# Queries unnormalised in the scores, with the inverse norm in the exponential of a windowed attention

## The chip, the core and the metric

The kernel runs on one core of one Trainium2 chip. A core has five engines with their own instruction streams: TensorE (PE, matrix products and transposes), VectorE (DVE), ScalarE (ACT, activations by table), GpSimd (POOL) and SyncE (SP, which issues transfers here). They meet through semaphores only. The metric is the device time of one execution in microseconds (us); lower is better.

## The reference

The input is x of 8 batches, 256 tokens and 128 channels. It is normalised over the channels; the result xn goes into two branches, and both are added to x. The first is a causal attention of 16 heads of 64. The second is a stack of six layers on xn:

```
for i in range(6):
    x = attn_layer(shift_tokens(x), Wqkv[i], q_scale[i], k_scale[i], Wo[i]) + x
    x = ffn_layer(shift_tokens(x), ln_g[i], ln_b[i], W1[i], b1[i], W2[i], b2[i]) + x
```

The attention layer of the stack is where the change is. Queries and keys of each head (64 long) are divided by their l2 norm, multiplied by learned scales, and rotated (`q*cos*scale + rotate_half(q)*sin*scale`). A window of 32 queries sees its own 32 keys and the 32 before, with a causal band. The scores are multiplied by 8, go through a softmax over the 64 keys, and weigh the values. The feed-forward layer is a LayerNorm, a product to 2 x 341 columns, a gate by the exact gelu, and a product back to 128.

## The kernel before

There are two stages. The first (to about 335 us) computes the causal branch and is not changed, but for two buffers of x that now lie elsewhere. The second, some 1600 us, is the stack. Its unit is one batch of one layer, 48 in all, and a unit has four groups of four heads: 192 groups. A pipeline written out by hand runs over 192 slots, one group entering per slot. In slot s the engines work on different groups at once: projections of keys, queries and values for group s+4, norms of group s+3 (the rotated queries and keys are moved by SP for group s+2), scores, softmax and weights of group s, weighing of the values and output projection for groups s-1 and s-2. LayerNorm parts come once every four slots and the MLP of two units once every eight: gate products in slots 5, 6 and 7 of a period of eight, the gelus in slot 0, the up products in 1, 2 and 3, the down product in 4. Every engine's `slot` function fixes its order, and waits in it are on semaphores with constant values.

What happens to one group before the change, on which engine:

- TensorE projects keys and queries into PSUM (`keys`, `queries`). ScalarE squares them (`squares`, line 621) and VectorE multiplies them with the rotary tables (`rotate`, lines 1310 and 1311); the queries are rotated after they are squared.
- GpSimd adds the halves of the squares (line 451), adds the rotary products (`rotated`, line 431, into `z_raw`), and multiplies keys and queries with the inverse norms (`normalise`, line 424, into `z_norm`), 512 columns each.
- TensorE sums the squares over the 32 partitions of a head with a block matrix (`norms`, line 958), 512 columns: 256 tokens of queries and 256 of keys. ScalarE takes Ln (line 690) and the exponential of minus one half of it (line 693); VectorE clamps (line 1390).
- SP copies the result in eight transfers into the layout for the scores, `zqk` (line 350).
- TensorE writes mask and scores into `pair_bank`, two banks of PSUM with 4 blocks of 64 keys each for 128 partitions (32 queries of four windows), `windows`, lines 965 and 974. VectorE takes the negative maximum of the eight blocks (line 1289) and adds it (line 1291), ScalarE takes one exponential of 512 columns in place (line 686), VectorE sums (1296), inverts (1298) and weighs (1301). TensorE transposes (line 984), ScalarE copies to `spread` (line 630), and TensorE weighs the values (line 996). ScalarE copies the output to `yt` (`output_out`, line 657), which TensorE projects (line 926).

ScalarE's other work in a slot: the values to SBUF (`values_out`, line 561), gate copies (715), gelus (663, 667) with a table load before (661) and after (681), the LayerNorm's Ln and exponential (636, 639), its squares (650) and gain (644). VectorE's: input split (1315, 1317), residuals (1325, 1345), hidden products (1353), LayerNorm copies (1332, 1337).

## Time and profile before

| | |
|---|---|
| median of 3 runs | 1941.88 us (1940.21 to 1942.47) |
| profiled execution, its own time | 1940.49 us |
| its span | 1938.7 us |
| mean granted TensorE clock | 0.999 of full |
| instructions | 68797 |
| PE busy in the span | 1851.4 us, x27097 |
| DVE, ACT, POOL busy | 1577.9, 1408.8, 1368.8 us |
| stage of the stack, by its scores | 335.8 to 1904.9 us |

Busy time is time in which an engine has at least one instruction under way; instructions on TensorE are pipelined and overlap in the records. "Idle before" is time in which the engine waited, with what ended the wait. A full-precision matmul shows as two records, a transpose as one. An instruction on VectorE or ScalarE can start before the record of the one ahead of it ends.

### The profile page before, as it was taken

The page shows a single profiled execution, that of the slowest core. Times are in us where ns is not written, and L with a number is a line of the kernel's source. Part 1 is how long each engine was busy: PE and PEld are TensorE (multiplying, and loading weights), DVE is VectorE, ACT ScalarE, POOL GpSimd, SP SyncE. Part 2 cuts the span into 40 slices and gives each one's busy share as a digit, 9 for nine tenths or more (in the row PEclk, how much of TensorE's full clock was granted, in tenths as well). Part 3 has the DMA queues.
Part 4 walks back from the last instruction along what each step waited for, and adds up shares of the span by engine and source line. Part 5 has one row for each costly group of instructions (what it writes and reads, how often), then busy time and mean ns, then how long its engine had stood idle before and what let it go on. Part 6 is the DMA issues. An engine that isn't in the chain of part 4 may idle for free.

```text
span 1938.7 us, 68797 instructions
## 1 busy us (share of the span) xinstructions
PE 1851.4 (95%) x27097; PEld 1394.4 (72%) x27097; DVE 1577.9 (81%) x3052; ACT 1408.8 (73%) x2853; POOL 1368.8 (71%) x1455
## 2 busy tenths in 40 slices
PE   6999998999999999999999999999999999999997
PEld 4777765777767777777777677777677776777774
DVE  5776777888888888788888888888888888888875
ACT  5766665677777777877777777778777777777784
POOL 3010025898798787888787987878887879888770
PEclk9999999999999999999999999999999999999999
DMA  4000001444434334334344343443333443433332
GB/s 131 2 1 0 0 0 39 105 105 103 127 85 110 94 101 128 93 93 104 96 104 123 87 107 97 103 126 94 93 103 96 108 120 88 107 96 102 94 98 67
DMA packets 193542, 171.07 MB, mean 88 GB/s; under 512 B 32304, under 2 KB 190168, under 8 KB 193240
## 3 DMA queue, kind: packets, MB, share of 16 engines
q1 hardware_dynamic: 193240, 166.89, 32.9%
q8 instruction: 209, 3.42, 0.8%
q14 instruction: 93, 0.76, 0.1%
HBM read 21.01 MB, written 1.05 MB: 11 GB/s over the span
## 4 chain that ended last, share of the span: by engine, by line
PE 71%; ACT 12%; issue 7%; DVE 4%; POOL 3%; SPq 3%; DMA 0%; ACTq 0%; POOLq 0%; DVEq 0%
PE bank L996 7%; PE bank L958 7%; PE bank L926 6%; PE pair_bank L974 6%; PE bank L1005 5%; PE bank L984 3%; PE bank L1057 3%; PE bank L1006 3%; PE bank L1007 3%; PE bank L1079 3%; ACT sq L621 2%; SPq L350 2%; PE bank L843 2%; PE bank L1071 2%; ACT probs L690 2%
## 5 line engine op out<-in xcount | busy, mean ns | idle before, releaser
L431 POOL TENSOR_TENSOR z_raw<-rot_u,rot_v 128x256 f32<-128x256 f32 x768 | 553.1, 744 | 100.9 <-DVE rot_v L1311 95.6
L424 POOL TENSOR_TENSOR z_norm<-probs_t,z_raw 128x512 f32<-128x512 f32 x376 | 481.8, 1282 | 92.1 <-DVE probs_t L1390 89.1
L1310 DVE TENSOR_TENSOR rot_u<-bank,tabs 128x512 f32<-128x512 f32 x384 | 263.1, 685 | 165.0 <-ACT sq L621 164.6
L451 POOL TENSOR_TENSOR sqs<-sq 128x512 f32<-128x512 f32 x192 | 246.1, 1282 | 90.0 <-issue 89.4
L1005 PE MATMUL bank<-x_high,w_high 128*128 128x256 f32 x768 | 301.2, 392 | 0.2 <-issue 0.2
L686 ACT ACTIVATE pair_bank<-pair_bank 128x512 f32<-128x512 f32 x192 | 111.7, 582 | 220.4 <-DVE pair_bank L1291 220.1
L1311 DVE TENSOR_TENSOR rot_v<-bank,tabs 128x512 f32<-128x512 f32 x384 | 261.4, 681 | 0.0
L621 ACT ACTIVATE sq<-bank 128x512 f32<-128x512 f32 x384 | 225.2, 588 | 49.8 <-PE bank L1007 43.6
L996 PEld LDWEIGHTS bank<-probs_t,v_late 128*64 128x64 f32 x3072 | 155.0, 137 | 144.4 <-issue 144.4
L630 ACT ACTIVATE probs_t<-bank 64x512 f32<-64x512 f32 x384 | 226.7, 590 | 35.7 <-PE bank L984 33.4
L958 PE MATMUL bank<-sqs,consts 128*128 128x512 f32 x384 | 198.8, 599 | 25.0 <-POOL sqs L451 25.0
L1006 PE MATMUL bank<-x_high,w_low 128*128 128x256 f32 x768 | 216.0, 281 | 0.0
L1007 PE MATMUL bank<-x_low,w_high 128*128 128x256 f32 x768 | 216.0, 281 | 0.0
L996 PE MATMUL bank<-probs_t,v_late 128*64 128x64 f32 x3072 | 198.8, 228 | 0.5 <-ACT probs_t L630 0.5
L926 PE MATMUL bank<-yt,wo 128*128 128x256 f32 x768 | 197.6, 380 | 0.0
L996 PE MATMUL bank<-probs_t,v_sb 128*64 128x64 f32 x3072 | 189.5, 222 | 0.0
L1005 PEld LDWEIGHTS bank<-x_high,w_high 128*128 128x128 f32 x768 | 144.6, 188 | 58.4 <-issue 38.9
L690 ACT ACTIVATE probs<-bank,tiny 128x512 f32<-128x512 f32 x188 | 129.2, 687 | 64.7 <-PE bank L958 62.1
L1289 DVE TENSOR_REDUCE nm<-pair_bank 128x8 f32<-128x512 f32 x192 | 132.1, 688 | 49.3 <-PE pair_bank L974 48.1
L1006 PEld LDWEIGHTS bank<-x_high,w_low 128*128 128x128 f32 x768 | 145.2, 189 | 36.9 <-issue 36.9
L974 PE MATMUL pair_bank<-zqk 64*32 64x64 f32 (+1 forms) x12288 | 163.9, 221 | 0.0
L974 PEld LDWEIGHTS pair_bank<-zqk 64*32 64x32 f32 x12288 | 132.7, 105 | 40.6 <-issue 40.4
(183 smaller groups left out, 4543.4 us busy)
## 6 DMA issues: line engine op xcount, KB each, us to landing
zqk<-z_norm SPq DMA_DIRECT2D x1536, 64.0 KB, 2.1
v_late<-v_sb SPq DMA_DIRECT2D x192, 192.0 KB, 2.6
w_qkv<-in_L_ffn_Wqkv SPq DMA_DIRECT2D x18, 512.0 KB, 4.9
v_late<-v_sb SPq DMA_DIRECT2D x192, 32.0 KB, 2.8
wo<-in_L_ffn_Wo SPq DMA_DIRECT2D x24, 128.0 KB, 2.3
w<-in_L_ffn_W SPq DMA_DIRECT2D x12, 170.5 KB, 2.6
z_norm<-in_L_attn_x SPq DMA_DIRECT2D x4, 256.0 KB, 5.5
w_qkv<-in_L_attn_w_kv_up SPq DMA_DIRECT2D x4, 256.0 KB, 5.0
```

The costliest lines, as they stand in the source:

```text
L424: return pool.tensor_tensor(z_norm[:, parity, idx, :, :], rinv(m)[:, idx, :].unsqueeze(1).broadcast_to([P, 2, T]), z_raw[:, parity, idx, : ...
L431: a = pool.tensor_tensor(z_raw[:, parity, idx, half, :], rot_u[:, idx, half, :], rot_v[:, idx, 1 - half, :], ALU.add)
L621: act.activation(sq[:, idx, :, :], src[:, :].rearrange("p (a t) -> p a t", a=2), ACT.Square).then_inc(S[mark], 1)
L926: mm = pe.matmul(B_X[:, 0:T], wo[:, c, :], yt[:, c, :], start=(c == 0), stop=(c == HD // P - 1))
L958: pe.matmul(B_N[:, :], con("blk"), sqs[:, :, :].rearrange("p a t -> p (a t)"), start=True, stop=True).then_inc(S["n_done"], 1)
L974: mm = pe.matmul(bank[a][WIN * tile:WIN * tile + WIN, at + skip:at + KEYS], zqk[rows, g, 0, pair, WIN * j:WIN * j + WIN], zqk[rows, g, 1, ...
L996: mm = pe.matmul(y[:, t, tile % 2, :, :], (v_sb if tile % 2 else v_late)[:, odd, t, f], spread[:, h, tile, :], start=True, stop=True, tile ...
L1005: pe.matmul(dst, w_high[:, j, cols], x_high[:, odd, :], start=True, stop=False)
L1006: pe.matmul(dst, w_low[:, j, cols], x_high[:, odd, :], start=False, stop=False)
L1007: mm = pe.matmul(dst, w_high[:, j, cols], x_low[:, odd, :], start=False, stop=True)
L1310: dve.tensor_tensor(rot_u[:, idx, :, :], src, tabs[:, 2 * idx, :, :], ALU.mult)
L1311: dve.tensor_tensor(rot_v[:, idx, :, :], src, tabs[:, 2 * idx + 1, :, :], ALU.mult).then_inc(S[mark], 1)
```

## The change

- The queries are no longer multiplied with their inverse norm. Rotated queries and keys go into one buffer, `zs`, of four groups; keys are normalised in place; queries go as they are.
- `squares` writes in another order, and GpSimd's sum likewise, so that the queries' sums lie as two blocks of 128 tokens.
- `norms` makes three products: 256 columns for the keys as before, and two in which the queries' squares are the stationary operand (128 x 128) and four columns of the block matrix move. Their result has one column per head and token block, with the queries' tokens along the partitions: 8 columns. Ln, exponential and clamp run on 256 + 8 columns; the clamp of the 8 goes to `q_rinv`, one for each of four groups.
- Since the inverse norm is positive, the softmax's maximum can be taken of the unnormalised scores. VectorE multiplies the 8 negative maxima with the 8 inverse norms (`lift`), in place of adding the maxima to the 512 scores.
- The exponential becomes eight instructions of 64 columns, with `q_rinv` as scale and `lift` as bias.
- ScalarE's order: the output copy goes ahead of the key squares; the gain of every second LayerNorm goes into the slot after the gelus; in the slot of the gelus both gelus go behind the query squares and behind the next group's values copy, which moves there from the next slot's beginning.
- GpSimd has no second `normalise`; SP waits for the rotated queries besides.

```
--- before.py
+++ after.py
@@ -40,6 +40,7 @@
 
 KEYS = 2 * WIN
 TILES = P // WIN
+NORMS = T + 2 * HG
 
 UNITS = DEPTH * NB
 GROUPS = UNITS * G
@@ -143,8 +144,9 @@
         rot_v = sb("rot_v", [P, 2, 2, T])
         sq = sb("sq", [P, 2, 2, T])
         sqs = sb("sqs", [P, 2, T])
-        z_raw = sb("z_raw", [P, 2, 2, 2, T])
-        z_norm = sb("z_norm", [P, 2, 2, 2, T])
+        zs = sb("zs", [P, G, 2, 2, T])
+        q_rinv = sb("q_rinv", [P, G, 2 * HG])
+        lift = sb("lift", [P, 2 * HG])
 
         zqk = sb("zqk", [P, G, 2, 2, T])
         v_sb = sb("v_sb", [P, 2, TT, HD])
@@ -152,14 +154,14 @@
         nm = sb("nm", [P, HG, TT])
 
 
-        x_rows = z_norm.rearrange("p g a b t -> p (g a b t)").rearrange("p (n c) -> p n c", c=P)
-        xn_rows = z_raw.rearrange("p g a b t -> p (g a b t)").rearrange("p (n c) -> p n c", c=P)
+        x_rows = zs[:, 2:4, :, :, :].rearrange("p g a b t -> p (g a b t)").rearrange("p (n c) -> p n c", c=P)
+        xn_rows = zs[:, 0:2, :, :, :].rearrange("p g a b t -> p (g a b t)").rearrange("p (n c) -> p n c", c=P)
         probs = sb("probs", [P, HG, 3 * P])
         probs_t = sb("probs_t", [P, HG, 3 * P])
         scored = probs.rearrange("p h c -> p (h c)")[:, 0:HG * 2 * KEYS].rearrange("p (a k r) -> p a k r", a=2, r=KEYS)
         spread = probs_t.rearrange("p h c -> p (h c)")[:, 0:HG * TILES * KEYS].rearrange("p (h s c) -> p h s c", h=HG, s=TILES)
-        late_ln = probs.rearrange("p h c -> p (h c)")[:, 2 * GW * 2:].rearrange("p (a t) -> p a t", a=2)
-        late_rinv = probs_t.rearrange("p h c -> p (h c)")[:, 2 * GW * 2:].rearrange("p (a t) -> p a t", a=2)
+        late_ln = probs.rearrange("p h c -> p (h c)")[:, 2 * GW * 2:2 * GW * 2 + NORMS]
+        late_rinv = probs_t.rearrange("p h c -> p (h c)")[:, 2 * GW * 2:2 * GW * 2 + NORMS]
         rsum = sb("rsum", [P, HG, TT])
         rrec = sb("rrec", [P, HG, TT])
         yt = sb("yt", [P, HD // P, T])
@@ -173,11 +175,11 @@
 
         def ln_n(m):
 
-            return late_ln if m >= G else gate[:, 0:2, 0:T]
+            return late_ln if m >= G else gate[:, 0, 0:NORMS]
 
         def rinv(m):
 
-            return late_rinv if m >= G else gate[:, 0:2, T:2 * T]
+            return late_rinv if m >= G else gate[:, 1, 0:NORMS]
 
 
         pair_bank = ctx.enter_context(nc.psum_tensor("pair_bank", [P, 2, 512], F32))
@@ -341,13 +343,14 @@
                 if active(s, -2, GROUPS - 2):
 
                     g = (s + 2) % G
+                    sp.wait_ge(S["q_summed"], s + 3)
                     sp.wait_ge(S["zn_ready"], s + 3)
                     if s + 2 < G:
                         sp.wait_ge(S["qk_done"], HG * (STEPS - G + s + 3))
                     for h in range(HG):
                         for half in range(2):
                             to = 64 * (h % 2) + 32 * half
-                            sp.dma_start(zqk[to:to + 32, g, :, h // 2, :], z_norm[32 * h:32 * h + 32, s % 2, :, half, :]).then_inc(S[f"z_in{g}"], 16)
+                            sp.dma_start(zqk[to:to + 32, g, :, h // 2, :], zs[32 * h:32 * h + 32, g, :, half, :]).then_inc(S[f"z_in{g}"], 16)
                 if active(s, -3, GROUPS - 3):
 
                     g, odd = (s + 3) % G, (s + 3) // G % 2
@@ -418,17 +421,17 @@
                 pool.wait_ge(S[high], count)
                 pool.tensor_tensor(w_low[:, :, cols], src[:, :, cols], w_high[:, :, cols].bitcast(F32), ALU.subtract).then_inc(S[done], 1)
 
-            def normalise(m, idx):
-
-                parity = m % 2
-                return pool.tensor_tensor(z_norm[:, parity, idx, :, :], rinv(m)[:, idx, :].unsqueeze(1).broadcast_to([P, 2, T]), z_raw[:, parity, idx, :, :], ALU.mult)
-
-            def rotated(m, parity, idx, prod, mark):
+            def normalise(m):
+
+                z = zs[:, m % G, 1, :, :]
+                return pool.tensor_tensor(z, rinv(m)[:, 0:T].unsqueeze(1).broadcast_to([P, 2, T]), z, ALU.mult)
+
+            def rotated(m, idx, prod, mark):
 
                 pool.wait_ge(S[prod], m + 1)
-                after(pool, "zn_ready", m - 1)
+                after(pool, f"z_in{m % G}", 16 * 2 * HG * (m // G))
                 for half in range(2):
-                    a = pool.tensor_tensor(z_raw[:, parity, idx, half, :], rot_u[:, idx, half, :], rot_v[:, idx, 1 - half, :], ALU.add)
+                    a = pool.tensor_tensor(zs[:, m % G, idx, half, :], rot_u[:, idx, half, :], rot_v[:, idx, 1 - half, :], ALU.add)
                 a.then_inc(S[mark], 1)
 
             def slot(s):
@@ -437,23 +440,21 @@
                     pool.wait_ge(S["pv_done"], STEPS)
                     pool.memset(spread[:, :, :, :], 0.0).then_inc(S["spread_zero"], 1)
                 if one:
-                    rotated(s + 4, s % 2, 1, "k_prod", "k_summed")
+                    rotated(s + 4, 1, "k_prod", "k_summed")
                 if two:
 
                     pool.wait_ge(S["bound_ready"], s + 4)
-                    after(pool, f"z_in{(s + 1) % G}", 16 * 2 * HG * ((s + 1) // G + 1))
                     pool.wait_ge(S["k_summed"], s + 4)
-                    normalise(s + 3, 1)
+                    normalise(s + 3).then_inc(S["zn_ready"], 1)
                 if one:
                     pool.wait_ge(S["k_square"], s + 5)
                     pool.wait_ge(S["q_square"], s + 5)
                     after(pool, "n_done", s + 4)
-                    pool.tensor_tensor(sqs[:, :, :], sq[:, :, 0, :], sq[:, :, 1, :], ALU.add).then_inc(S["sums_ready"], 1)
-                if two:
-                    pool.wait_ge(S["q_summed"], s + 4)
-                    normalise(s + 3, 0).then_inc(S["zn_ready"], 1)
+                    parts = sq.rearrange("p i a t -> p (i a t)").rearrange("p (n a c) -> p n a c", a=2, c=P)
+                    total = sqs.rearrange("p i t -> p (i t)").rearrange("p (n c) -> p n c", c=P)
+                    pool.tensor_tensor(total, parts[:, :, 0, :], parts[:, :, 1, :], ALU.add).then_inc(S["sums_ready"], 1)
                 if one:
-                    rotated(s + 4, s % 2, 0, "q_prod", "q_summed")
+                    rotated(s + 4, 0, "q_prod", "q_summed")
                 for g in range(G):
                     l = layer_begun(s, LAYER - 7 + g)
                     if l:
@@ -618,7 +619,9 @@
             def squares(m, done, src, idx, mark):
                 act.wait_ge(S[done], m + 1)
                 after(act, "sums_ready", m)
-                act.activation(sq[:, idx, :, :], src[:, :].rearrange("p (a t) -> p a t", a=2), ACT.Square).then_inc(S[mark], 1)
+                n = (4, 2)[idx]
+                dst = sq[:, idx, :, :].rearrange("p a t -> p (a t)").rearrange("p (x n c) -> p n x c", x=2, n=n)
+                act.activation(dst, src[:, :].rearrange("p (n x c) -> p n x c", x=2, n=n), ACT.Square).then_inc(S[mark], 1)
 
             def spread_out(n):
 
@@ -671,7 +674,7 @@
                 one, two = active(s, -4, GROUPS - 4), active(s, -3, GROUPS - 3)
                 three, four = active(s, 0, GROUPS), active(s, 1, GROUPS + 1)
                 normed = g == 0 and active(s, 2 * G, 2 * G + GROUPS)
-                if two and s >= 0:
+                if two and s >= 0 and not mlp_slot(s, 17):
                     values_out(s + 3)
                 if s == 1:
                     act.wait_ge(S["spread_zero"], 2)
@@ -683,14 +686,20 @@
                     deviations((s - 8) // G, B_M)
                 if three:
                     act.wait_ge(S["shifted"], s + 1)
-                    act.activation(both, both, ACT.Exp).then_inc(S["raised"], 1)
+                    for a in range(2):
+                        for k in range(4):
+                            at = 4 * a + k
+                            m = act.activation(both[:, a, k, :], both[:, a, k, :], ACT.Exp, bias=lift[:, at:at + 1], scale=q_rinv[:, g, at:at + 1])
+                    m.then_inc(S["raised"], 1)
                 if two:
                     m = s + 3
                     act.wait_ge(S["n_done"], m + 1)
-                    act.activation(ln_n(m), B_N[:, :].rearrange("p (a t) -> p a t", a=2), ACT.Ln, bias=tiny[:, 0:1], scale=LNS).then_inc(S["ln_done"], 1)
+                    act.activation(ln_n(m), B_N[:, 0:NORMS], ACT.Ln, bias=tiny[:, 0:1], scale=LNS).then_inc(S["ln_done"], 1)
                     act.wait_ge(S["ln_done"], m + 1)
                     after(act, "zn_ready", m)
                     act.activation(rinv(m), ln_n(m), ACT.Exp, scale=-0.5).then_inc(S["rinv_ready"], 1)
+                if four:
+                    output_out(s - 1)
                 if one:
                     squares(s + 4, "k_prod", B_K, 1, "k_square")
                 l = layer_begun(s, LAYER - 5)
@@ -703,22 +712,22 @@
                     rotary_tables(l, 0)
                 if g == 3 and active(s, 7, 7 + GROUPS):
                     xc_squares((s - 7) // G)
-                if normed:
+                if normed and s % (2 * G) == G:
                     gained((s - 8) // G)
-                if four:
-                    output_out(s - 1)
+                if s % (2 * G) == 1 and active(s, 9, 9 + GROUPS):
+                    gained((s - 9) // G)
                 for c in range(3):
                     if mlp_slot(s, 13 + c):
                         p = (s - 13 - c) // (2 * G)
                         act.wait_ge(S["gate_done"], 3 * p + c + 1)
                         after(act, "hid_ready", 3 * p + c - 2)
                         act.activation(gate[0:CW[c], c, :], B_M[0:CW[c], :], ACT.Identity, bias=gate_bias[0:CW[c], c:c + 1]).then_inc(S["gate_ready"], 1)
-                session = mlp_slot(s, 16)
-                if session:
-                    gelus((s - 16) // (2 * G))
                 if one:
                     squares(s + 4, "lq_done", B_Q, 0, "q_square")
-                if session:
+                if mlp_slot(s, 16):
+                    if active(s + 1, -3, GROUPS - 3):
+                        values_out(s + 4)
+                    gelus((s - 16) // (2 * G))
                     last_gelus((s - 16) // (2 * G))
                 l = layer_begun(s, LAYER + 6)
                 if l:
@@ -955,7 +964,12 @@
                 if m == 0:
                     pe.wait_ge(S["res_done"], NB - 1)
                 pe.wait_ge(S["sums_ready"], m + 1)
-                pe.matmul(B_N[:, :], con("blk"), sqs[:, :, :].rearrange("p a t -> p (a t)"), start=True, stop=True).then_inc(S["n_done"], 1)
+                pe.matmul(B_N[:, 0:T], con("blk"), sqs[:, 1, :], start=True, stop=True)
+                heads = con("blk").rearrange("p (b a c) -> p a b c", b=2, a=2)[:, :, :, 0]
+                for x in range(2):
+                    dst = B_N[:, T:NORMS].rearrange("p (a b x) -> p x a b", a=2, b=2)[:, x, :, :]
+                    mm = pe.matmul(dst, sqs[:, 0, P * x:P * x + P], heads, start=True, stop=True)
+                mm.then_inc(S["n_done"], 1)
 
             def windows(n, unit, g):
 
@@ -1283,12 +1297,13 @@
             def by_block(a):
                 return a[:, :, :].rearrange("p (a b) x -> p a (b x)", a=2)
 
-            def shift_windows(n):
+            def lift_windows(n):
 
                 dve.wait_ge(S["scores_done"], n + 1)
                 dve.tensor_reduce(by_block(nm), both, AX_X, ALU.max, negate=True).then_inc(S["top_ready"], 1)
                 dve.wait_ge(S["top_ready"], n + 1)
-                dve.tensor_tensor(both, both, by_block(nm).unsqueeze(3).broadcast_to([P, 2, 4, KEYS]), ALU.add).then_inc(S["shifted"], 1)
+                after(dve, "raised", n)
+                dve.tensor_tensor(lift[:, :], nm.rearrange("p h t -> p (h t)"), q_rinv[:, n % G, :], ALU.mult).then_inc(S["shifted"], 1)
 
             def weigh_down(n):
 
@@ -1378,7 +1393,7 @@
                 if g == 3 and active(s, 7, 7 + GROUPS):
                     centred_out((s - 7) // G)
                 if three:
-                    shift_windows(s)
+                    lift_windows(s)
                 if one:
                     rotate(s + 4, 1, B_K, "lk_done", "k_summed", "k_prod")
                 if g == 0 and active(s, 8, 8 + GROUPS):
@@ -1387,7 +1402,9 @@
                     weigh_down(s)
                 if two:
                     dve.wait_ge(S["rinv_ready"], s + 4)
-                    dve.tensor_scalar(rinv(s + 3), rinv(s + 3), 1e12 / ROOT, None, ALU.min).then_inc(S["bound_ready"], 1)
+                    after(dve, "raised", s)
+                    dve.tensor_scalar(q_rinv[:, (s + 3) % G, :], rinv(s + 3)[:, T:NORMS], 1e12 / ROOT, None, ALU.min)
+                    dve.tensor_scalar(rinv(s + 3)[:, 0:T], rinv(s + 3)[:, 0:T], 1e12 / ROOT, None, ALU.min).then_inc(S["bound_ready"], 1)
                 if s == 0:
                     dve.wait_ge(S["wo_done"], NB + 1)
                     dve.tensor_copy(attn[:, NB - 1, :], B_Y[:, 0:T]).then_inc(S["res_done"], 1)
```

## Rows read from the trace of the kernel before

**Rows 1.** The page, part 1: busy time and share of each engine.

```profile
PE 1851.4 (95%) x27097; PEld 1394.4 (72%) x27097; DVE 1577.9 (81%) x3052; ACT 1408.8 (73%) x2853; POOL 1368.8 (71%) x1455
```

**Rows 2.** Busy time, one period: window, us, PE, PEld, DVE, ACT, POOL, clock, DMA.

```profile
988.02:1053.60 65.58, 64.31 (x1036) 48.86 (x1034) 55.26 (x99) 49.79 (x87) 52.60 (x57) 1.00 0.44 118
```

**Rows 3.** Timeline of PE, end of that period: start us, us, engine, line, operation.

```profile
1053.25 0.60 PE L984 MATMUL bank<-consts,probs 128*128 128x128 f32 x4
1053.68 0.38 PE L965 MATMUL pair_bank<-mask_local_b,ident_b 128*128 128x256 bf16 x2
```

**Rows 4.** Timeline of ACT in a slot with a gate copy: columns as in Rows 3.

```profile
1033.80 0.58 ACT L686 ACTIVATE pair_bank<-pair_bank 128x512 f32<-128x512 f32 x1 [2.44 <-DVE pair_bank L1291]
1034.41 0.69 ACT L690 ACTIVATE probs<-bank,tiny 128x512 f32<-128x512 f32 x1
...
1035.66 0.58 ACT L621 ACTIVATE sq<-bank 128x512 f32<-128x512 f32 x1
1036.14 0.59 ACT L657 ACTIVATE yt<-bank 128x512 f32<-128x512 f32 x1
1036.62 0.69 ACT L715 ACTIVATE gate<-bank,gate_bias 128x512 f32<-128x512 f32 x1
1037.19 0.61 ACT L621 ACTIVATE sq<-bank 128x512 f32<-128x512 f32 x1
...
1038.14 1.19 ACT L630 ACTIVATE probs_t<-bank 64x512 f32<-64x512 f32 x2
1040.49 0.58 ACT L686 ACTIVATE pair_bank<-pair_bank 128x512 f32<-128x512 f32 x1 [1.16 <-DVE pair_bank L1291]
```

**Rows 5.** Timeline of DVE in that slot.

```profile
1032.34 0.69 DVE L1289 TENSOR_REDUCE nm<-pair_bank 128x8 f32<-128x512 f32 x1
1033.07 0.70 DVE L1291 TENSOR_TENSOR pair_bank<-pair_bank,nm 128x512 f32<-128x512 f32 x1
...
1034.87 0.68 DVE L1296 TENSOR_REDUCE rsum<-pair_bank 128x8 f32<-128x512 f32 x1
...
1036.02 0.69 DVE L1301 TENSOR_TENSOR probs<-pair_bank,rrec 128x512 f32<-128x512 f32 x1 [0.23 <-DVE rrec L1298]
...
1036.96 0.85 DVE L1345 TENSOR_TENSOR xs<-bank,xs 64x256 f32<-64x256 f32 x2
1037.84 0.69 DVE L1310 TENSOR_TENSOR rot_u<-bank,tabs 128x512 f32<-128x512 f32 x1
...
1039.05 0.68 DVE L1289 TENSOR_REDUCE nm<-pair_bank 128x8 f32<-128x512 f32 x1
```

**Rows 6.** Groups of ACT by form: count, busy us, mean ns, idle before.

```profile
L644 ACT ACTIVATE xh<-xc,gain 128x256 f32<-128x256 f32 x48 | 28.4, 592 | 0.9 <-DVE xc L1337 0.9
...
L650 ACT ACTIVATE xc<-xc 128x256 f32<-128x256 f32 x48 | 19.5, 407 | 0.9 <-DVE xc L1332 0.9
...
L540 ACT ACTIVATE probs<-pair_bank,nm 128x128 f32<-128x128 f32 x64 | 23.5, 367 | 7.9 <-DVE nm L1236 7.9
```

**Rows 7.** Timeline of PE: output projection, then norms.

```profile
1031.81 1.03 PE L926 MATMUL bank<-yt,wo 128*128 128x256 f32 x4
1032.67 1.02 PE L958 MATMUL bank<-sqs,consts 128*128 128x512 f32 x2
```

**Rows 8.** Groups of DVE by form, as Rows 6.

```profile
L1317 DVE TENSOR_TENSOR x_low<-xs,x_high 128x256 fp32r<-128x256 f32 x48 | 61.6, 1284 | 1.7
...
L1325 DVE SCALAR_TENSOR_TENSOR xs<-bank,out_bias,xs 64x512 f32<-64x512 f32 x46 | 34.3, 746 | 4.4 <-PE bank L1175 2.5 <-PE bank L1079 1.6
L1353 DVE SCALAR_TENSOR_TENSOR hid<-bank,out_bias,gate 128x512 f32<-128x512 f32 x44 | 32.9, 747 | 0.7
```

**Rows 9.** Timeline of ACT in the slot of the gelus.

```profile
990.74 0.58 ACT L686 ACTIVATE pair_bank<-pair_bank 128x512 f32<-128x512 f32 x1 [0.37 <-DVE pair_bank L1291]
991.83 0.69 ACT L690 ACTIVATE probs<-bank,tiny 128x512 f32<-128x512 f32 x1 [0.51 <-PE bank L958]
...
1000.89 0.58 ACT L686 ACTIVATE pair_bank<-pair_bank 128x512 f32<-128x512 f32 x1
```

95 lines of the change are left out of this document (56 added, 39 removed).

## The prediction

> **What bounds the kernel now.** I read the page's busy shares first, then one period of the second stage, then the timelines of ScalarE and VectorE in one slot. TensorE is busy for 95% of the span [rows 1]. The second stage is 192 slots in 24 periods of eight (a pair of MLP blocks goes through in eight slots). The period from the mask product at 988.02 to the one at 1053.68 takes 65.66 us [rows 2, 3], and in it TensorE is busy for 64.31 us, VectorE 55.26, ScalarE 49.79 and GpSimd 52.60 [rows 2]. So TensorE sets the pace and the others wait for it in most slots. ScalarE has 16 us per period to spare, 2 us per slot. That is the number to watch, for the change puts seven more instructions per slot on ScalarE.
>
> In a slot without a gelu ScalarE starts the exponential at 1033.80, the Ln at 1034.41, the key squares at 1035.66, and the next exponential at 1040.49, having idled for 1.16 us [rows 4]. VectorE reduces at 1032.34, shifts, sums at 1034.87, weighs at 1036.02, and reduces again at 1039.05: 6.71 us with almost no idle time, 0.88 of them the residual at 1036.96 [rows 5]. These two engines form a ring: exponential, Ln and its exponential, squares of the keys, squares of the queries (ScalarE), rotation of the queries, maximum, shift (VectorE), exponential. Today it has slack against TensorE. The question is its length after the change. I call the time from one slot's first exponential to the next slot's a ring step.
>
> **The exponentials.** One instruction of 512 columns (0.58 us, the next 0.61 after its start) becomes eight of 64, each with a scale and a bias read from SBUF. The trace has no such instruction. The nearest: 128 columns out of PSUM with a bias from SBUF take 367 ns; a 256-column one with both operands takes 592 against 407 with neither, so 93 ns for each operand [rows 6]. 512 columns without either take 0.58 [rows 4], 367 less 93 is 274 for 128, so a column costs 0.80 ns. 64 columns with both: 367 - 51 + 93 = 409 ns. Instructions that follow each other overlap by 0.10 (squares 0.58 long, the next 0.48 later [rows 4]), so they start 0.31 apart, and the eight take 7 x 0.31 + 0.41 = 2.58. Bounds: 0.20 apart, if the operands are read under the instruction before (lower), and 0.41, if nothing overlaps. The upper end is real: the present exponential, the one instruction of ScalarE that writes PSUM, has no overlap with the one behind it (0.61 from start to start [rows 4]). I take 0.31, because 64-column instructions into one bank depend on nothing before them, and every other chained group overlaps.
>
> By the Trainium skill, "ScalarE: Activation LUTs", on what an ACTIVATE costs, an instruction is 186 ns plus 0.833 ns per column plus 93 ns for each pointer operand, and neighbours overlap by 93. An estimate from that is 0.33 apart, 2.75 for the eight; the sum below would be about 2042 by it. The trace agrees on the 93 ns of an operand.
>
> **What is taken off.** Ln and its exponential shrink from 512 to 264 columns, 0.20 each: from Ln to squares 0.84 instead of 1.25 [rows 4]. The shift on VectorE (0.70 from PSUM to PSUM) becomes a product of 8 columns, some 0.20 (at least 0.1, at most the 0.70); the first exponential starts 0.96 after the reduction instead of 1.46 [rows 5]. The clamp becomes two smaller ones, nought net (between -0.2 and +0.1). GpSimd loses the query normalisation, one of its four steps a slot; it has 13 us per period of idle time already [rows 2], and its sums, 1.3 behind the query squares, are wanted only in the next slot. SP keeps its eight transfers per slot, and the added wait on the query sums is met a slot before (they end on GpSimd one slot ahead of the key normalisation that SP waits for anyway), so the transfers start no later.
>
> **TensorE.** The norm product of 512 columns loses its half: four records of 256 columns take 0.86 [rows 7], so 256 columns of full precision are 0.43. In return come two products with 128-column weights and 4 moving columns, two records each: four weight loads. The four transposes of a slot, a load and 128 columns each, take 0.43 from 1053.25 to 1053.68 [rows 3], so a load is at most 0.11. One load lies under the product ahead; 0.33 to 0.36 stays. Net -0.07 per slot (between -0.35 and +0.05). Off TensorE's path this is worth nothing, on it 13 us.
>
> **The ring after the change**, from first exponential to the next, for a bare slot: to the Ln 2.61, Ln and exponential 0.84, output copy 0.48 (now ahead of the squares, on the ring), key squares 0.48, query squares 0.61; that is 5.02. Then rotation 1.21, reduction 0.72, lift 0.24: 7.19. VectorE's own way is 2.62 to the sum (it idles 1.4 behind the key rotation; the exponential used to hide there), then 1.15 to the weighing and 0.75 with the clamp scaled down [rows 5], so at 4.52 it is free, and 2.17 more make 6.69. Extras: gate copy 0.57 [rows 4], residual 0.88 [rows 5], input split 1.7 with its cast, MLP residual 1.53 for two, hidden product 0.66 [rows 8], centred copy 0.35. By slot of the period (0 has the gelus):
>
> - 0: today 10.15, all ScalarE but for a wait of 0.51 [rows 9]; +2.00 for the exponentials, -0.41 Ln, -0.51 wait gone, -0.49 gain [rows 6] moved to slot 1: 10.7
> - 1: 4.52 + 0.88 + 0.66 + 2.17 = 8.2
> - 2: 4.52 + 0.66 + 2.17 + 0.35 = 7.7
> - 3: ScalarE's own load, 2.61 + 0.84, four of 0.48, 0.31 for the centred squares [rows 6], 1.2 for the spread copies [rows 4] and 0.93 for the LayerNorm's Ln and exponential of 256 columns (by the column rate): 7.8
> - 4: 4.52 + 1.7 + 2.17 + 1.53 = 9.9
> - 5, 6: 7.19 + 0.57 = 7.8, and 8.1 with the centred copy
> - 7: the same with a gate copy: 8.4
>
> The sum is 68.6 against 65.66. TensorE's own work is 64.31 [rows 2], so the ring leads and TensorE waits for weights in most slots. 2.9 x 24 = 70 us on the profiled execution's 1940.5 (span 1938.7): 2010, and 1.4 more against the median of 1941.88: **2012**. The first stage doesn't change.
>
> **Sensitivity.** 0.01 us in the spacing is 0.08 in each of the slots, 15 us in all. 0.28 gives 1965, 0.34 gives 2058: the forecast's own range.
>
> **Rivals.**
> 1. *No overlap between exponentials* (0.41 apart, as the present one stands to its successor). Ring +0.8 per slot, +154: about 2165. For it: the 0.61 of rows 4. Against: its successor is another function with a wait of its own.
> 2. *The change is faster.* The operands are fetched under the instruction before, 0.20 apart. Then the ring is 68.6 - 8 x 0.88 = 61.5 per period and TensorE sets it: 64.31 busy [rows 2], less 0.56 for the norms, plus half of the 1.27 that it idles today (the query rotation no longer stands behind the gelus, which is where sums come late): 64.4, -1.3 x 24 = -31: about 1910. It decides below a spacing of 0.26 (2.9 us in eight slots is 0.36 per slot, 0.045 per exponential). For it: VectorE and ScalarE have slack today. Against: the 93 ns of an operand show in the spacing too: behind the gate copy with its bias (0.69 long) the next starts 0.57 later, behind a plain square (0.58) 0.48 later [rows 4].
> 3. *In between*, 0.25 to 0.27: 1940 to 1955, where ring and TensorE tie.
>
> A change that doesn't do what it says (norms not halved in time) is in the TensorE bounds and moves nothing where the ring leads.
>
> **Chances.** Forecast 0.45, rival 1 0.27, rival 2 0.16, rival 3 0.12 (of which 0.05 within 0.2%, 0.01 below). A measurement of this kernel tells 0.2% from no change. Faster 0.17, same 0.05, slower 0.78. The range from 1935 to 2170 leaves out rival 2 and the tail above rival 1.
>
> **What would show it.** In the changed profile: eight exponentials of about 0.41, 0.31 apart; VectorE idle before the sum of the weights (line 1296 now) for some 1.4 us, released by ScalarE, near nil today; TensorE idle before the transposes, released by VectorE's weights; ScalarE over 90% busy; TensorE under 93%. The norm products' step falls from 0.86 to about 0.8. If the exponentials start 0.25 apart or less, or TensorE stays at 95%, the forecast is wrong. If they are 0.40 apart, rival 1 holds. If the period is long with exponentials at 0.31, the ring isn't the cause, and I would look at GpSimd's sums and the values' wait for the Ln.

## The result and the profile after

The changed kernel takes 2051.78 us (median of 4 runs, 2049.37 to 2054.73) against 1941.16 (1940.21 to 1942.47, 4 runs): ratio 1.057, 95% interval 1.0552 to 1.0588. It is slower by 110.6 us; the forecast was 2012, slower by 70. The profiled execution has a span of 2050.4 us at a granted clock of 0.998 of full speed, so the clock plays no part.

The page of the changed kernel, part 1 (busy us, share of the span, instructions; it answers to [rows 1]):

```profile
PE 1864.0 (91%) x27865; PEld 1520.5 (74%) x27865; DVE 1477.5 (72%) x3244; ACT 1668.8 (81%) x4197; POOL 1132.3 (55%) x1263
```

ScalarE gains 260 us of busy time, VectorE loses 100 and GpSimd 236. TensorE is nearly as busy as before in us, but over a longer span: 91% instead of 95%. So it waits more. Part 4 of the same page, the chain that ended last (shares by engine, then by line):

```profile
ACT 38%; PE 30%; DVE 19%; issue 11%; DMA 0%; ACTq 0%; POOL 0%; DVEq 0%; SPq 0%
ACT pair_bank L692 18%; DVE nm L1303 4%; ACT sq L624 3%; PE pair_bank L988 3%; DVE rot_v L1326 2%; DVE rsum L1311 2%; PE bank L1093 2%; PE bank L998 2%; ACT probs L697 2%; ACT probs_t L633 2%; ACT gate L724 2%; DVE hid L1368 2%; PE bank L852 2%; DVE lift L1306 2%; PE bank L1115 2%
```

The eight exponentials (L692) are 18% of that chain, and ScalarE and VectorE together are 57% of it. It is the ring: exponentials, squares, rotation, maximum (L1303), lift (L1306). Part 5 of the page, two of its groups (busy us, mean ns, then idle time before them with what ended it):

```profile
L692 ACT ACTIVATE pair_bank<-pair_bank,lift,q_rinv 128x64 f32<-128x64 f32 x1536 | 469.3, 387 | 143.3 <-DVE lift L1306 143.0
...
L1311 DVE TENSOR_REDUCE rsum<-pair_bank 128x8 f32<-128x512 f32 x192 | 132.7, 691 | 289.9 <-ACT pair_bank L692 289.9
```

An exponential of 64 columns takes 387 ns (409 forecast). VectorE stands idle for 290 us ahead of the sum of the weights, always for the last exponential.

One slot of ScalarE, 1012.52 to 1020.28 (timeline: start us, us, engine, line, operation, count; in brackets the idle time before it and what ended it). It answers to [rows 4]:

```profile
1012.52 2.44 ACT L692 ACTIVATE pair_bank<-pair_bank,lift,q_rinv 128x64 f32<-128x64 f32 x8 [1.91 <-DVE lift L1306]
1015.00 0.48 ACT L697 ACTIVATE probs<-bank,tiny 128x264 f32<-128x264 f32 x1
...
1015.84 0.58 ACT L660 ACTIVATE yt<-bank 128x512 f32<-128x512 f32 x1
...
1016.79 0.69 ACT L724 ACTIVATE gate<-bank,gate_bias 128x512 f32<-128x512 f32 x1
1017.36 0.61 ACT L624 ACTIVATE sq<-bank 128x512 f32<-128x512 f32 x1
...
1020.28 2.45 ACT L692 ACTIVATE pair_bank<-pair_bank,lift,q_rinv 128x64 f32<-128x64 f32 x8 [0.77 <-DVE lift L1306]
```

Eight exponentials take 2.44 us from start to end, so they start (2.44 - 0.39) / 7 = 0.29 apart (0.31 forecast). The next such block starts 7.76 us later, a ring step of slot 5 (7.8 forecast). The other blocks of this period start at 1002.20, 1028.71, 1037.33, 1047.86, 1055.87, 1064.30 and 1072.73. Against the forecast:

| slot | 4 | 5 | 6 | 7 | 0 | 1 | 2 | 3 | sum |
|---|---|---|---|---|---|---|---|---|---|
| forecast | 9.9 | 7.8 | 8.1 | 8.4 | 10.7 | 8.2 | 7.7 | 7.8 | 68.6 |
| measured | 10.32 | 7.76 | 8.43 | 8.62 | 10.53 | 8.01 | 8.43 | 8.43 | 70.53 |

The period was 65.66 [rows 3]. Every fourth period is longer, before and after: a layer begins in it, and it went from 69.3 to 72.76 us (starts of the exponentials in both timelines). Between the first block of exponentials and the one 23 periods later, five of them of the long kind, the kernel grew by 104.3 us (18 times 4.87 and five times 3.4 are 105). With 1.6 ahead of it and 5.7 behind it that is the 111.7 us by which the span grew. The busy times in this period, which answer to [rows 2] (window, us, PE, PEld, DVE, ACT, POOL, clock, DMA share, GB/s):

```profile
1002.20:1072.73 70.53, 64.88 (x1067) 54.03 (x1067) 51.53 (x107) 60.48 (x144) 43.05 (x48) 1.00 0.43 115
```

No engine is full: ScalarE 60.48 of 70.53 (86%; I had said over 90%), TensorE 92%. The time is in their dependence on each other.

The forecast's steps with 2.45 in place of 2.58 for the exponentials would sum to 68.6 - 8 x 0.13 = 67.6. The kernel needs 70.5, so 2.9 us of the period (about 70 us in all) were missing from the forecast. Over the slots as they were forecast, slots 2 and 3 are long by 0.73 and 0.63, slot 4 by 0.42, slot 6 by 0.33 and slot 7 by 0.22. What TensorE waited for tells where (the changed kernel's waits of TensorE; us in total, times, longest):

```profile
PE bank L1031 <- ACT probs L697: 32.6, 29, 2.2
PE bank L1107 <- DVE hid L1368: 29.7, 22, 1.7
PE bank L1010 <- ACT probs_t L633: 21.9, 23, 1.0
PE bank L1107 <- ACT gate L724: 21.2, 23, 1.1
PE bank L1115 <- ACT gate L724: 14.1, 23, 1.9
PE bank L998 <- DVE probs L1316: 13.1, 53, 2.1
```

The largest row is the values' product (L1031). It waits for the Ln in slot 1, behind the gelus of slot 0, and neither of these slots is longer than forecast. I had forecast waits of the transposes (L998) for the weights in most slots; that is the last and smallest row. L1107 and L1115 are the two small LayerNorm products (mean and variance) of slots 2, 3, 6 and 7. They write the PSUM bank that the MLP uses too, so they wait until VectorE has read the hidden product out of it (L1368) or ScalarE the gate (L724). The transposes, the mask and the scores stand behind L1107 in TensorE's order and start only after it. Slot 2, TensorE then VectorE (timelines):

```profile
1061.08 0.67 PE L1107 MATMUL bank<-xs,consts 128*128 128x256 f32 x2 [1.23 <-DVE hid L1368]
1061.59 0.60 PE L998 MATMUL bank<-consts,probs 128*128 128x128 f32 x4
1062.03 0.38 PE L979 MATMUL pair_bank<-mask_local_b,ident_b 128*128 128x256 bf16 x2
1062.34 0.84 PE L988 MATMUL pair_bank<-zqk 64*32 64x32 f32 x64
```

```profile
1058.35 0.69 DVE L1311 TENSOR_REDUCE rsum<-pair_bank 128x8 f32<-128x512 f32 x1 [1.32 <-ACT pair_bank L692]
...
1059.31 0.69 DVE L1316 TENSOR_TENSOR probs<-pair_bank,rrec 128x512 f32<-128x512 f32 x1
...
1060.19 0.75 DVE L1368 SCALAR_TENSOR_TENSOR hid<-bank,out_bias,gate 128x512 f32<-128x512 f32 x1
...
1063.21 0.69 DVE L1303 TENSOR_REDUCE nm<-pair_bank 128x8 f32<-128x512 f32 x1 [0.75 <-PE pair_bank L988]
1063.94 0.32 DVE L1306 TENSOR_TENSOR lift<-nm,q_rinv 128x8 f32<-128x8 f32 x1
```

The late exponentials hold back the sum, the sum the weighing, the weighing the hidden product, and that holds TensorE for 1.23 us. So the scores come late, and VectorE idles another 0.75 for them. That is a second, longer ring through TensorE, which my sum over ScalarE and VectorE didn't have.

The lift has no fixed price either. It is 0.32 here, 0.17 and 0.44 elsewhere; the last section shows what sets it.

### The profile page after: what moved, and what is told of

It is laid out like the page before. It is cut to its first block, busy times and chain, and to the rows that moved or that the text cites. A ratio compares the mean times of both kernels' runs of the same rounds, so it can differ in the third digit from the quotient of the medians.

```text
span 2050.4 us, 72240 instructions
## 1 busy us (share of the span) xinstructions
PE 1864.0 (91%) x27865; PEld 1520.5 (74%) x27865; DVE 1477.5 (72%) x3244; ACT 1668.8 (81%) x4197; POOL 1132.3 (55%) x1263
## 4 chain that ended last, share of the span: by engine, by line
ACT 38%; PE 30%; DVE 19%; issue 11%; DMA 0%; ACTq 0%; POOL 0%; DVEq 0%; SPq 0%
ACT pair_bank L692 18%; DVE nm L1303 4%; ACT sq L624 3%; PE pair_bank L988 3%; DVE rot_v L1326 2%; DVE rsum L1311 2%; PE bank L1093 2%; PE bank L998 2%; ACT probs L697 2%; ACT probs_t L633 2%; ACT gate L724 2%; DVE hid L1368 2%; PE bank L852 2%; DVE lift L1306 2%; PE bank L1115 2%
## 5 line engine op out<-in xcount | busy, mean ns | idle before, releaser
L434 POOL TENSOR_TENSOR zs<-rot_u,rot_v 128x256 f32<-128x256 f32 x768 | 548.7, 736 | 224.8 <-DVE rot_v L1326 221.6
L692 ACT ACTIVATE pair_bank<-pair_bank,lift,q_rinv 128x64 f32<-128x64 f32 x1536 | 469.3, 387 | 143.3 <-DVE lift L1306 143.0
L427 POOL TENSOR_TENSOR zs<-probs_t,zs 128x512 f32<-128x512 f32 x188 | 239.7, 1275 | 373.3 <-DVE probs_t L1407 373.3
L1311 DVE TENSOR_REDUCE rsum<-pair_bank 128x8 f32<-128x512 f32 x192 | 132.7, 691 | 289.9 <-ACT pair_bank L692 289.9
L455 POOL TENSOR_TENSOR sqs<-sq 128x512 f32<-128x512 f32 x192 | 250.4, 1304 | 30.1 <-issue 27.5
L1303 DVE TENSOR_REDUCE nm<-pair_bank 128x8 f32<-128x512 f32 x192 | 131.9, 687 | 56.7 <-PE pair_bank L988 53.3
L1010 PEld LDWEIGHTS bank<-probs_t,v_sb 128*64 128x64 f32 x3072 | 158.7, 138 | 1.0 <-issue 1.0
```

Of the source, the lines that this page charges most:

```text
L427: return pool.tensor_tensor(z, rinv(m)[:, 0:T].unsqueeze(1).broadcast_to([P, 2, T]), z, ALU.mult)
L434: a = pool.tensor_tensor(zs[:, m % G, idx, half, :], rot_u[:, idx, half, :], rot_v[:, idx, 1 - half, :], ALU.add)
L455: pool.tensor_tensor(total, parts[:, :, 0, :], parts[:, :, 1, :], ALU.add).then_inc(S["sums_ready"], 1)
L692: m = act.activation(both[:, a, k, :], both[:, a, k, :], ACT.Exp, bias=lift[:, at:at + 1], scale=q_rinv[:, g, at:at + 1])
L1010: mm = pe.matmul(y[:, t, tile % 2, :, :], (v_sb if tile % 2 else v_late)[:, odd, t, f], spread[:, h, tile, :], start=True, stop=True, tile ...
```

## The experiments

All of them are the changed kernel or the kernel before with one edit. Ratios are against the kernel before on the same chip (1941 to 1942 us).

**1. One exponential.** One instruction of 512 columns again, with a constant scale; the inverse norm and the shift are still computed but not applied.

```diff
-    for a in range(2):
-        for k in range(4):
-            m = act.activation(both[:, a, k, :], ..., ACT.Exp, bias=lift[:, at:at + 1], scale=q_rinv[:, g, at:at + 1])
+    act.activation(both, both, ACT.Exp, scale=1e-30)
```

> The changed kernel with its eight exponentials of 64 columns put back to one of 512, with no bias and no scale from SBUF (a tiny constant scale; the lift and the inverse norm are left out of the softmax). Theory, the exponentials on the ring set the changed kernel's time: without them ScalarE gives back about 1.9 us per slot, the ring falls under TensorE's work, and the time is below before, 1905 to 1930 us. Rival, the slowdown comes from the other parts (SP's added wait, the order of ScalarE, the small products): it stays above 1990 us.

Measured: 1891.75 us (1889.56 to 1894.03), ratio 0.9749 (0.9732 to 0.9765). TensorE is busy for 97% of the span:

```profile
PE 1822.6 (97%) x27865; PEld 1513.3 (80%) x27865; DVE 1470.1 (78%) x3244; ACT 1358.7 (72%) x2853; POOL 1138.9 (60%) x1263
```

It is 13 us below the range that I had given it. The eight exponentials with their operands cost 160.0 us, and all else in the change gives back 49.4. The loss is theirs alone.

This run also shows what a slot costs without the ring. Its slots 3 and 7 take 7.9 and 8.07 us (medians of the periods), and slot 4 takes 10.36, as long as in the change. The same slot 4 in the kernel before, in the changed kernel and in this one (columns as in the window above):

```profile
1023.33:1033.80 10.47, 10.47 (x141) 7.02 (x141) 9.03 (x16) 5.62 (x10) 7.17 (x8) 1.00 0.42 105
```

```profile
1002.20:1012.52 10.32, 10.32 (x144) 8.20 (x143) 8.55 (x17) 6.98 (x18) 5.51 (x6) 1.00 0.38 95
```

```profile
1001.98:1012.36 10.38, 10.38 (x145) 8.25 (x143) 8.44 (x17) 5.32 (x12) 5.49 (x6) 1.00 0.39 101
```

TensorE is busy for all of it in all three. Slot 4 is TensorE's own, whatever the exponentials cost, and the trace before the change showed it: I forecast 9.9 for a slot that took 10.47.

**2. The norm product.** As 1, with the norm product of 512 columns in place of its half and the two small ones (the norms that it gives are then not those wanted).

```diff
-    pe.matmul(B_N[:, 0:T], con("blk"), sqs[:, 1, :], ...)      # and two with 4 moving columns
+    pe.matmul(B_N[:, :], con("blk"), sqs[:, :, :]...)
```

> As one_exp, and with the norm product of TensorE put back to one of 512 columns (the small sums of the queries are then not what they should be). With TensorE as the bound, this measures the norm edit by itself. Theory: the four weight loads of the new products eat what the halved product gives, so the two kernels are within 0.3% (6 us) of each other. Rival, the halving saves its 0.3 us and more per slot: this one is 50 us slower than one_exp.

Measured: 1901.07 us, ratio 0.9796 (0.9779 to 0.9812), so halving is worth 9.3 us where TensorE leads, 0.049 per slot. My theory had allowed 6 and the rival wanted 50: nearer to the theory, but outside of it. TensorE in experiment 1, then in this one (timelines, norm product to the next product):

```profile
1002.51 0.59 PE L963 MATMUL bank<-sqs,consts 128*128 128x256 f32 x2
1002.94 0.50 PE L967 MATMUL bank<-consts,sqs 128*128 128x4 f32 x4
1003.37 0.34 PE L1006 MATMUL bank<-probs_t,v_late 128*64 128x64 f32 x4
```

```profile
1006.25 1.02 PE L963 MATMUL bank<-sqs,consts 128*128 128x512 f32 x2
1007.20 0.34 PE L1001 MATMUL bank<-probs_t,v_late 128*64 128x64 f32 x4
```

0.86 against 0.95 from start to start: the half product takes 0.43 and the small ones, four weight loads for 16 columns, another 0.43.

**3. The order alone.** The kernel before with the change's order of ScalarE (output copy ahead of the key squares, query squares ahead of the gelus, value copy and gain moved).

```diff
+    if four: output_out(s - 1)
     if one: squares(s + 4, "k_prod", B_K, 1, "k_square")
...
-    if session: gelus(...)
     if one: squares(s + 4, "lq_done", B_Q, 0, "q_square")
+    if mlp_slot(s, 16): values_out(s + 4); gelus(...)
```

> The kernel before with ScalarE's new order alone. Theory: the query squares no longer stand behind the long gelu, so the sums come in time and TensorE's wait in the gelu slots shrinks: 1915 to 1935 us, a little faster than before. Rival, the order is a cost of its own (the output copy ahead of the key squares delays the rotation): 1950 us or more.

Measured: 1928.14 us, ratio 0.9935 (0.9918 to 0.9951): 13 us gained. The kernel before and this one, TensorE's wait for GpSimd's sums of squares:

```profile
PE bank L958 <- POOL sqs L451: 25.0, 28, 1.3
```

```profile
PE bank L960 <- POOL sqs L451: 6.4, 6, 1.2
```

The query squares no longer stand behind the gelus, and 18.6 us of this wait go; other waits take back some. This is the gain that rival 2 had named.

**4. Eight exponentials alone.** The kernel before; VectorE's shift goes into the bias, the scale is a tile of ones.

```diff
-    dve.tensor_tensor(both, both, by_block(nm)..., ALU.add).then_inc(S["shifted"], 1)
...
-    act.activation(both, both, ACT.Exp)
+    for a in range(2):
+        for k in range(4):
+            m = act.activation(both[:, a, k, :], ..., ACT.Exp, bias=top[:, at:at + 1], scale=unit[:, at:at + 1])
```

> The kernel before with only its exponential changed: eight of 64 columns, the negative maximum as bias and a column of ones as scale, both from SBUF, and no shift on VectorE. Everything else, norms, normalisation on GpSimd and order, is as before. Theory, the exponentials alone make the slowdown: 2035 to 2090 us (the Ln is longer and the gelu slot is in its old order, so rather above the changed kernel's 2052). Rival, the slowdown needs the other parts: below 1990 us.

Measured: 2071.61 us, ratio 1.0672 (1.0654 to 1.069), 130 us slower, though VectorE is spared 0.70 us per slot. So the exponentials do it without the norms, the order or the rest. They take the same time here (groups of ScalarE: busy us, mean ns):

```profile
L694 ACT ACTIVATE pair_bank<-pair_bank,nm,unit 128x64 f32<-128x64 f32 x1536 | 468.6, 386 | 106.8 <-DVE nm L1299 106.5
```

**5. Eight without operands, and 6. with one.** The changed kernel; the exponentials have a constant scale, with no bias (5) or with the lift as bias (6). The inverse norm isn't applied in either, nor the maximum in 5.

```diff
-    m = act.activation(both[:, a, k, :], ..., ACT.Exp, bias=lift[:, at:at + 1], scale=q_rinv[:, g, at:at + 1])
+    m = act.activation(both[:, a, k, :], ..., ACT.Exp, scale=1e-30)                          # 5
+    m = act.activation(both[:, a, k, :], ..., ACT.Exp, bias=lift[:, at:at + 1], scale=1e-30)  # 6
```

> The changed kernel with its eight exponentials of 64 columns kept, but with a constant scale and no bias, so without operands from SBUF (the lift and the inverse norm are left out of the softmax). By the plain form's own numbers (0.58 us for 512 columns, 0.80 ns a column) one takes 0.22 us and the eight start 0.11 to 0.12 apart, about 1.0 us in all, 1.4 less than with the operands. Theory, the price is the operands' on the ring: 1890 to 1910 us, near one_exp's 1892. Rival, it is the number of instructions: above 1970 us.

> The changed kernel with a constant scale in its eight exponentials, so one operand from SBUF (the bias) instead of two; the inverse norm is left out as scale. The two ends are measured: 2.44 us for eight with both operands (2052 us), and eight without any (1901 us). Theory: each operand adds 0.09 to every start, so these start 0.20 apart, 1.7 us in all, 0.74 less per slot than with both; the ring falls to about TensorE's work: 1910 to 1940 us. Rival, an operand's cost comes once however many there are: 2030 us or more.

Measured: 5 takes 1900.66 us, ratio 0.9788 (0.9772 to 0.9804); 6 takes 1943.15, ratio 1.0004 (0.9994 to 1.0014), 3 us above the range that I had given it. One block of each (timelines of ScalarE), 5 first:

```profile
1016.20 1.02 ACT L692 ACTIVATE pair_bank<-pair_bank 128x64 f32<-128x64 f32 x8 [1.90 <-DVE lift L1306]
```

```profile
1008.31 1.72 ACT L692 ACTIVATE pair_bank<-pair_bank,lift 128x64 f32<-128x64 f32 x8 [1.10 <-DVE lift L1306]
```

1.02, 1.72 and 2.44 us with none, one and two operands: each costs some 0.70 us in eight instructions, 0.09 in one. Being eight costs only 8.9 us of the kernel's time (1891.75 to 1900.66). The first operand costs 42.5 and the second 108.6, though both add about 0.7 x 192 = 135 us to ScalarE: the slack that the ring had against TensorE takes up most of the first and little of the second. The price per instruction is linear, the kernel's time is not.

**7. The MLP's bank freed early.** The changed kernel; the hidden product is read out of its bank ahead of the weighing on VectorE, the gate copy is put ahead of the output copy on ScalarE.

```diff
     dve.reciprocal(...)
+    if mlp_slot(n, 17 + c): hidden_out(p, c, B_M, ...)
     dve.tensor_tensor(scored, ...)
...
+    if mlp_slot(s, 13 + c): act.activation(gate[0:CW[c], c, :], B_M[0:CW[c], :], ...)
     if four: output_out(s - 1)
```

> The changed kernel with bank 3 released earlier: on VectorE the hidden product goes ahead of the weighing, on ScalarE the gate copy goes ahead of the output copy. The LayerNorm's product on TensorE waits for these, and the transposes and scores stand behind it. Theory, in slots 2, 3, 6 and 7 the ring is closed through TensorE by that wait: each gets 0.4 to 0.7 us shorter, 2005 to 2025 us. Rival, only the ring of ScalarE and VectorE counts (as the prediction had it): swapping inside it leaves its length, 2045 us or more.

Measured: 2047.65 us (2041.81 to 2053.84), ratio 1.0548 (1.0518 to 1.0578). A miss: I expected 2005 to 2025, and against the change's 1.057 (1.0552 to 1.0588) the gain isn't clear of the noise. Slots 1 to 3 (ScalarE's timeline; the block after slot 0 starts at 1043.31):

```profile
1051.72 2.45 ACT L692 ACTIVATE pair_bank<-pair_bank,lift,q_rinv 128x64 f32<-128x64 f32 x8 [1.51 <-DVE lift L1306]
1059.44 2.44 ACT L692 ACTIVATE pair_bank<-pair_bank,lift,q_rinv 128x64 f32<-128x64 f32 x8 [0.98 <-DVE lift L1306]
1067.39 2.43 ACT L692 ACTIVATE pair_bank<-pair_bank,lift,q_rinv 128x64 f32<-128x64 f32 x8
```

Slots 2 and 3 fall from 8.43 and 8.43 to 7.72 and 7.95, as the second ring says they should. But slot 1 rises from 8.01 to 8.41. The hidden product starts there at once, and the weights come 0.66 us later for it. What lengthens the slot is the lift: it took 0.19 in the change and takes 0.60 here, up to 1051.68, just behind the end of a GpSimd instruction at 1051.66 (timelines of VectorE and GpSimd; the last section shows more of this):

```profile
1051.09 0.60 DVE L1306 TENSOR_TENSOR lift<-nm,q_rinv 128x8 f32<-128x8 f32 x1
```

```profile
1050.93 1.41 POOL L434 TENSOR_TENSOR zs<-rot_u,rot_v 128x256 f32<-128x256 f32 x2
```

(That row holds two instructions; the first of them is the one that ends at 1051.66.) Slots 6 and 7 stay at 8.44 and 8.62. TensorE no longer waits for the gate copy there, but in slot 7 it waits 1.20 for the centred squares, which now stand behind the gate copy on ScalarE, where it had waited 0.55 for the copy. So freeing the bank helped in two slots of eight, not in four.

The ordinary period is 69.8 us, 0.73 less than the change's, which would be some 17 us. But ten of the first 23 periods hold a stretch of 3.4 or 6.8 us in which TensorE was granted half its clock, 1.2 in place of 2.4 GHz. In the changed kernel none of the 23 does. One of them and the time before it (windows, columns as above):

```profile
1187.00:1192.50 5.50, 3.38 (x28) 2.43 (x24) 2.62 (x7) 5.43 (x15) 0.58 (x2) 1.00 0.38 103
1192.50:1195.90 3.40, 3.40 (x77) 2.76 (x75) 3.04 (x6) 1.90 (x5) 3.40 (x4) 0.51 0.10 24
```

Eight of the ten begin in slot 1 and two in slot 3. Ahead of this one TensorE had been busy for 3.38 of 5.50 us; in the same stretch of slot 1 in the changed kernel it is busy for 4.04 (1047.53 to 1053.03). It now waits 0.86 for the late weights there, in place of 0.21. An ordinary period with 3.4 us of half clock takes 70.2 to 70.7, the one with 6.8 us 72.4. The longest takes 74.6. In its slot 3 the scores came late at half clock, and then the lift took 1.64 us, up to the end of a GpSimd instruction that splits weights (the ends being 1427.03 and 1427.02):

```profile
1425.39 1.64 DVE L1306 TENSOR_TENSOR lift<-nm,q_rinv 128x8 f32<-128x8 f32 x1
```

```profile
1425.21 1.81 POOL L422 TENSOR_TENSOR w_low<-w_qkv,w_high 128x768 fp32r<-128x768 f32 x1
```

That the late weights brought on the falls of the clock is read from this trace. Periods without a fall have the same wait, so it doesn't decide alone. It fits that experiment 9, which leaves the first hidden product where it was, has none in its first 23 periods.

**8. VectorE's gap filled.** The changed kernel; the residual and the split of the input go into the time in which VectorE waits for the exponentials.

```diff
+    residual(...); split_input(...)
     if three: weigh_down(s)
```

> The changed kernel with VectorE's input split (1.7 us, slots 0 and 4) and residual (0.88 us, slots 1 and 5) moved ahead of the sum of the weights, into the 1.3 us that VectorE waits there for the exponentials. Theory: slot 4 and slot 1 get shorter where VectorE is last; slot 0 is ScalarE's own and gains nothing; 2020 to 2045 us. Rival, VectorE's way isn't the longer one in any slot: no change, 2048 to 2055 us.

Measured: 2042.78 us, ratio 1.0516 (1.0498 to 1.0533), 9 us better than the change. Slot 1 falls from 8.01 to 7.76, 6 us in 24 periods; the first period, while the pipeline fills, is 3.9 us shorter. Slot 4, for which the split was moved, stays at 10.34: as experiment 1 shows, it is TensorE's.

**9. Both.** As 8, and the hidden product early for the second and third block only; slot 1 keeps its order.

```diff
+    residual(...); split_input(...)
+    for c in (1, 2):
+        if mlp_slot(n, 17 + c): hidden_out(p, c, B_M, ...)
```

> The changed kernel with the input split and the residual in VectorE's gap, as in gap_filled, and the second and third hidden products ahead of the weighing; the gate copies and the first hidden product stay where they are. Theory: in slots 2 and 3 the ring is closed through TensorE (sum, weighing, hidden product, LayerNorm product behind it, scores): the two slots give back 0.5 to 0.7 each, as they did in early_release, without its late first hidden product; 2010 to 2030 us. Rival: what early_release gained was chance, 2038 to 2045 us.

Measured: 2021.17 us, ratio 1.0413 (1.0396 to 1.043), 30.6 us better than the change. Slots 1 to 3, of 7.76, 7.73 and 7.97:

```profile
1030.61 2.45 ACT L692 ACTIVATE pair_bank<-pair_bank,lift,q_rinv 128x64 f32<-128x64 f32 x8
1038.37 2.45 ACT L692 ACTIVATE pair_bank<-pair_bank,lift,q_rinv 128x64 f32<-128x64 f32 x8 [0.84 <-DVE lift L1306]
1046.10 2.45 ACT L692 ACTIVATE pair_bank<-pair_bank,lift,q_rinv 128x64 f32<-128x64 f32 x8 [0.98 <-DVE lift L1306]
1054.07 2.43 ACT L692 ACTIVATE pair_bank<-pair_bank,lift,q_rinv 128x64 f32<-128x64 f32 x8
```

With the second ring open, slots 2 and 3 are where the forecast had put them (7.7 and 7.8). 0.25 + 0.70 + 0.46 is 1.41 us of the period, 34 us in 24 periods, against 30.6 measured.

**10. The norm and the maximum on VectorE.** The changed kernel with one plain exponential; VectorE adds the maximum and multiplies by the inverse norm over all 512 columns. The full computation.

```diff
-    dve.tensor_tensor(lift, nm..., q_rinv[:, n % G, :], ALU.mult)
+    dve.tensor_tensor(both, both, by_block(nm)..., ALU.add)
+    dve.tensor_tensor(both, both, q_rinv[:, n % G, :]..., ALU.mult)
...
+    act.activation(both, both, ACT.Exp)
```

> The whole computation, with the inverse norm taken off ScalarE: VectorE adds the negative maximum and multiplies with the inverse norm in two passes over the 512 columns (0.6 us each, one more than before the change), and ScalarE takes one exponential of 512. Theory: ScalarE is as free as in one_exp, VectorE has 1.2 us per slot more than there and still fits under TensorE; 1895 to 1930 us, faster than before. Rival, VectorE's longer chain becomes the ring: 1950 us or more.

Measured: 1931.56 us, ratio 0.9947 (0.9931 to 0.9964), 1.6 us above the range that I had given it. The same job costs two VectorE passes of 0.70 us in place of eight exponentials, and the kernel is 120 us faster than the change.

**11. The same with the hidden product early** (all three blocks), and **12. the order alone with it** (the second and the third block).

```diff
+    if mlp_slot(n, 17 + c): hidden_out(p, c, B_M, ...)
     dve.tensor_tensor(scored, ...)
```

> two_passes with the hidden products ahead of the weighing on VectorE, the whole computation. TensorE's largest wait there is the LayerNorm product behind a hidden product, 18.7 us in 1200 (17 times, 1.1 at most). Theory: most of these 25 us over the stage go, 1905 to 1922 us. Rival: the hidden product now waits for its own product on TensorE and the weights come later by as much, 1928 us or more.

> order_only with the second and third hidden products ahead of the weighing on VectorE, the whole computation. TensorE waits 7.2 us in 1200 for hidden products there. Theory: 1918 to 1926 us, some 5 less than order_only. Rival: weights come later instead, 1928 us or more.

Measured: 1917.16 us (1916.24 to 1919.15), ratio 0.9877 (0.9861 to 0.9894), and 1924.41, ratio 0.991 (0.9893 to 0.9926). Experiment 11 beats both kernels of this case with the full computation. Its largest waits of TensorE in the window 400 to 1600:

```profile
PE bank L994 <- DVE probs L1318: 12.8, 31, 0.8
...
PE bank L1006 <- ACT probs_t L633: 7.5, 17, 0.5
```

The waits on the MLP's bank are gone from the top. Freeing it early is worth 14.4 us with two passes on VectorE (11 against 10), where TensorE had waited 18.7 us for hidden products in that window. With the order alone it gives 3.7 (12 against 3), of a wait of 7.2, and the two intervals overlap.

## Why the prediction was right, and where it was not

- **The direction and the mechanism hold.** Experiment 1 puts the whole loss on the exponentials, experiment 4 finds it again without the rest of the change, and three slots (5, 1, 0) stand at 7.76, 8.01 and 10.53 against 7.8, 8.2 and 10.7.
- **The exponentials** were slightly overrated: 387 ns and 0.29 apart for 409 and 0.31, so 2.45 and not 2.58. By the Trainium skill, "ScalarE: Activation LUTs", section "What ACT_TABLE_LOAD costs", an estimate is 0.33 apart. The trace disagrees on that, and agrees on the operand: 93 ns there, (2.44 - 1.02) / 16 = 0.089 us here. The sum by that estimate, 2042, lies nearer to the measured time than mine, but only because a larger error in the spacing hides more of what was missing elsewhere.
- **Rival 1 (no overlap) falls.** Eight exponentials in a row overlap, though all of them write PSUM. Why the old exponential and its successor, the Ln, stood 0.61 apart [rows 4] is not settled. In the changed kernel the Ln starts 0.03 after the end of the last exponential in most slots, but in slots 0 and 4 it starts 0.12 before it, so the change of function alone doesn't do it.
- **Rival 2 and rival 3** needed a spacing under 0.27. Experiment 6, with 1.72 for eight (0.20 apart, (1.72 - 0.30) / 7), shows what they would have come to: 1943 us, at rival 3's level and not at the 1910 of rival 2. Their point of decision was put too high: at 0.20 apart the kernel is no faster. Its slots 0 and 4 take 10.06 and 10.36, so a saving per slot can't be taken eight times over.
- **The failed term is the ring's length in slots 2 and 3 ("7.7", "7.8").** I had closed the ring through ScalarE and VectorE alone and made the transposes wait for weights. It closes through TensorE's queue and the MLP's bank too: 8.43 in both, 7.73 and 7.97 when the bank is freed in time (9). These 1.16 us are 28 of the missing 70. With the shorter exponentials counted, 0.46 more are over in the two slots, of which the lift can account for 0.24.
- **Slot 4 was never the ring's.** The sum took the ring's 9.9 for it, but it is full of TensorE's work (10.47, 10.32 and 10.38 us in the windows under experiment 1). With the shorter exponentials counted that is 0.55 of the period, 13 us in all. The step behind this is "so the ring leads": it compared the two sums over a period, 68.6 and 64.31, where the longer of the two has to be taken slot by slot.
- **Slots 6 and 7** are over by 0.46 and 0.35, counted the same way. In slot 6 the exponential starts 0.47 after the lift does, not 0.24, and the maximum waits 0.14 for the scores. In slot 7 ScalarE's queue waits 0.32 for the transposes. These two were read from the trace and not tested by themselves.
- **The lift was mis-sized.** I took 0.20 us between 0.1 and 0.7; it took 0.275 on average, 14 us in 192 slots, and I gave it one price for all slots where GpSimd's instructions set it slot by slot (last section).
- **The small steps.** The norm products' step fell from 0.95 to 0.86; I had read 0.86 as the step before and wanted 0.80 after. The gain was the 0.07 forecast to within 0.02. ScalarE over 90% was wrong (86% in the period); TensorE under 93% and VectorE's idle 1.4 ahead of the sum were right (91%; 289.9 / 192 = 1.5 at most, 1.32 in the slot shown).
- **Two errors partly cancelled.** With exponentials at 2.45, the forecast's own sum would have been 67.6, +47 us. It came within 2% because they were overrated, and that is luck.
